# Causal scores, maxima and masks contracted over 32 rows of the array instead of 64

## The reference

```
q, k, v = split(x @ w_qkv);  q, k rotated by position
att = (q @ k^T) * 8**-0.5            # per head, 1024 x 1024
att = where(causal, att, -max)
y = softmax(att) @ v;  x = x + y @ w_proj
```

## Time and profile before

| | |
|---|---|
| median of 3 runs | 667.92 us |
| lowest, highest | 662.89, 1288.06 us |
| span of the profiled execution | 665.4 us |
| PE busy | 603.9 us (91%) |
| DVE busy | 476.5 us (72%) |
| ACT busy | 348.3 us (52%) |
| POOL busy | 161.6 us (24%) |
| instructions | 12374 |

### The profile page before, as it was taken

One profiled execution on the slowest core, in us unless ns is written; L12 is line 12 of the kernel. 1 busy time (PEld: TensorE's weight loads), 2 busy tenths in 40 slices (PEclk: granted clock), 3 DMA queues, 4 the chain that ended last, 5 costly groups with the idle time before them and its releaser, 6 DMA issues. The chain is left out here.

```text
span 665.4 us, 12374 instructions
## 1 busy us (share of the span) xinstructions
PE 603.9 (91%) x4296; PEld 419.6 (63%) x4296; DVE 476.5 (72%) x1493; ACT 348.3 (52%) x713; POOL 161.6 (24%) x332
## 2 busy tenths in 40 slices
PE   1997789999989969999999999989999998999997
PEld 0876668788878855654545454545454535888887
DVE  5577866688786768958787878777888422876764
ACT  3855456322324644657676777755777674323321
POOL 7640524020033437702223121222120000000000
PEclk9998989999989996759999999995999987999999
DMA  8000000324322200000000000000000001333332
GB/s 292 4 0 1 1 0 1 91 85 126 119 66 86 75 1 1 1 0 1 2 1 1 1 2 2 1 1 1 1 1 1 1 1 66 88 122 117 120 122 75
DMA packets 18669, 27.98 MB, mean 42 GB/s; under 512 B 2984, under 2 KB 7208, under 8 KB 18608
## 3 DMA queue, kind: packets, MB, share of 16 engines
q1 hardware_dynamic: 17888, 25.85, 12.2%
q10 hardware_dynamic: 720, 1.34, 0.6%
HBM read 25.85 MB, written 1.33 MB: 41 GB/s over the span
## 5 line engine op out<-in xcount | busy, mean ns | idle before, releaser
L831 ACT ACTIVATE arena<-bank 128x512 f32<-128x512 f32 (+3 forms) x384 | 166.7, 496 | 76.6 <-PE bank L1664 51.6
L1686 PE MATMUL bank<-kza,qta 64*128 64x512 f32 (+3 forms) x384 | 141.7, 447 | 7.0 <-DVE work L1201 3.5
L1198 DVE CUSTOM_DVE_ANT_0 bank<-bank,mask_qk 128x512 f32<-128x512 f32 (+3 forms) x256 | 119.5, 517 | 36.7 <-PE bank L1686 36.3
L1652 PE MATMUL bank<-qtb,kza 64*128 64x512 f32 (+3 forms) x384 | 138.1, 431 | 4.4 <-ACT arena L831 2.2
L1686 PEld LDWEIGHTS bank<-kza,qta 64*128 64x128 f32 x384 | 67.3, 204 | 84.9 <-DVE work L1198 45.5
L761 ACT ACTIVATE work<-bank 128x512 f32<-128x512 f32 x80 | 47.8, 597 | 113.6 <-PE bank L1321 113.6
L1201 DVE TENSOR_REDUCE work<-bank 128x1 f32<-128x512 f32 x128 | 80.3, 683 | 17.0 <-PE bank L1686 17.0
L1124 DVE TENSOR_TENSOR work<-work,bank 128x512 f32<-128x512 f32 x80 | 54.8, 685 | 47.4 <-PE bank L1321 42.6
L1609 PE MATMUL bank<-arena 128*9 128x512 f32 (+3 forms) x768 | 86.7, 526 | 0.4 <-ACT arena L831 0.4
L1652 PEld LDWEIGHTS bank<-qtb,kza 64*128 64x128 f32 x384 | 67.7, 199 | 29.9 <-ACT arena L831 18.1
L1540 PE MATMUL bank<-dw,work 128*128 128x128 f32 x640 | 85.7, 278 | 0.7 <-DVE work L1128 0.7
(11 more groups left out here) (193 smaller groups left out, 1053.0 us busy)
## 6 DMA issues: line engine op xcount, KB each, us to landing
kt<-cw_rows SPq DMA_DIRECT2D x160, 128.0 KB, 2.9
x<-x_in SPq DMA_DIRECT2D x4, 256.0 KB, 7.6
y_out<-x SPq DMA_DIRECT2D x4, 256.0 KB, 3.2
arena<-gw_in SPq DMA_DIRECT2D x1, 640.0 KB, 9.8
arena<-uw_in SPq DMA_DIRECT2D x1, 640.0 KB, 8.6
dw<-dw_in SPq DMA_DIRECT2D x1, 640.0 KB, 9.5
work<-q_in SPq DMA_DIRECT2D x2, 256.0 KB, 8.1
arena<-const_in ACTq DMA_DIRECT2D x1, 400.0 KB, 7.3
```

The lines of the kernel that those rows point to most:

```text
L831: act.activation(pb[:, blk % 2, h, 0:w], s_bank(n)[:, 0:w], ACT.Exp, scale=SCALE).then_inc(p_ready, 1)
L1198: ins = dve.tensor_tensor_reduce(out=src, in0=src, in1=mask_qk[:, CW - w:], scale=1.0, scalar=-3e38, op0=ALU.add, op1=ALU.max, accum_out=dst)
L1652: ins = pe.matmul(s_bank(n)[:, 0:w], kz(s, h, j // CT)[pair(h), j % CT * P:(j % CT + 1) * P], qtb[pair(h), s % 2, (c + 1) * CW - w:(c + 1) ...
L1686: pe.matmul(a_bank(n)[:, 0:w], qta[pair(h), slot(b, g), i * P:(i + 1) * P], kz(s, h, half)[pair(h), 0:w], start=True, stop=True).then_inc( ...
```

## The change

Scores and maxima contract over a head's own 32 rows, straight from `kt`. `kza`, its two memsets, all copies by `alone` on ACT and POOL, and all waits for `kz_ready` are gone. The four heads use four row parts of the array. The orders of the heads and `BLOCK_ORDER` change with it. The mask is now four slices of 32 columns contracted over 32 rows, in place of two slices of 64 over 64, so `mask_kq` is twice as wide, the input of constants grows from 800 to 1056 columns, and there are 1024 mask matmuls in place of 512. The masks of the heads of order 0 and 1 are written as one group, slice by slice in turn. `gb` is a tile of its own.

```
-S_HEADS, A_HEADS = (0, 2, 1, 3), (2, 0, 3, 1)
-BLOCK_ORDER = (("score", 0), ("max", 0), ("max", 1), ("score", 1), ("mask", 0), ("mask", 1), ("score", 2),
-               ("max", 2), ("mask", 2), ("sums", None), ("max", 3), ("score", 3), ("mask", 3))
+S_HEADS, A_HEADS = (0, 1, 2, 3), (2, 3, 0, 1)
+BLOCK_ORDER = (("score", 0), ("max", 0), ("score", 1), ("max", 1), ("mask", (0, 1)), ("score", 2), ("max", 2),
+               ("mask", (2,)), ("sums", None), ("score", 3), ("max", 3), ("mask", (3,)))
...
-    for h in range(GH):
-        put("act", -1, 3, "alone", 0, 1, h)
-        put("act", -1, 7, "alone", 1, 1, h)
...
-    for s in range(2, STEPS):
-        put("pool", s - 2, 7, "alone", s, 0)
-        put("pool", s - 1, 0, "alone", s, 1)
...
-    for h in range(GH):
-        put("act", c2 + 16, "alone", 0, 0, h)
-        put("act", c2 + 18, "alone", 1, 0, h)
...
-        kza = sb("kza", [P, 4, 2, CW], F32R)
-        gb = kt[:, G:G + 2, :].bitcast(F32).rearrange("p g (a n) -> p (g a) n", a=2)
+        gb = sb("gb", [P, 4, CW])
...
-        def pair(h):
-
-            return slice(h // 2 * 2 * SL, (h // 2 + 1) * 2 * SL)
+        def own_rows(h):
+
+            return slice(h * SL, (h + 1) * SL)
...
-                if r == NC:
-                    sp.wait_ge(kz_ready[STEPS - 2], 2 * GH)
-                    sp.wait_ge(kz_ready[STEPS - 1], 2 * GH)
...
-                    ins = pe.matmul(s_bank(n)[:, 0:w], kz(s, h, j // CT)[pair(h), j % CT * P:(j % CT + 1) * P],
-                                    qtb[pair(h), s % 2, (c + 1) * CW - w:(c + 1) * CW], start=True, stop=True)
+                    r = own_rows(h)
+                    ins = pe.matmul(s_bank(n)[:, 0:w], kt[r, slot(b, g), j * P:(j + 1) * P],
+                                    qtb[r, s % 2, (c + 1) * CW - w:(c + 1) * CW], start=True, stop=True)
...
+                    for a in range(GH):
+                        for order in orders:
+                            n = (s * NBLK + k) * GH + order
+                            r = own_rows(S_HEADS[order])
+                            ins = pe.matmul(s_bank(n)[:, a * SL:(a + 1) * SL], mask_kq[r, a, :], identb[r, r],
                                             start=False, stop=True, skip_group_check=True)
+                            if a == GH - 1:
+                                ins.then_inc(b_full, 1)
...
-                    if order == 0 and k in (0, 8):
-                        pe.wait_ge(kz_ready[s], GH * (1 + half))
...
-                    pe.matmul(a_bank(n)[:, 0:w], qta[pair(h), slot(b, g), i * P:(i + 1) * P],
-                              kz(s, h, half)[pair(h), 0:w], start=True, stop=True).then_inc(a_full, 1)
+                    r = own_rows(h)
+                    pe.matmul(a_bank(n)[:, 0:w], qta[r, slot(b, g), i * P:(i + 1) * P],
+                              kt[r, slot(b, g), half * CW:half * CW + w], start=True, stop=True).then_inc(a_full, 1)
```

More of the change, by code:

```diff
@@ L49 @@
 W_Q, W_KV, W_QKV, W_R, W_END = 0, 128, 384, 768, 786
-C_ID, C_MA, C_MB, C_BM, C_HS, C_IO, C_COS, C_SIN, C_END = 0, 128, 256, 512, 640, 656, 672, 736, 800
+C_ID, C_MA, C_MB, C_BM, C_HS, C_IO, C_COS, C_SIN, C_END = 0, 128, 256, 768, 896, 912, 928, 992, 1056
 S_S1, S_B1, S_GA, S_BE, S_CW, S_CB, S_END = 0, 4, 8, 9, 10, 13, 14
@@ L216, in macaron @@
         identb = sb("identb", [P, P], BF16)
-        mask_kq = sb("mask_kq", [P, 2, P], BF16)
+        mask_kq = sb("mask_kq", [P, GH, P], BF16)
         mask_qk = sb("mask_qk", [P, CW], BF16)
@@ L339, in macaron @@
             sem("qkv_full"), sem("qkv_ready"), sem("v_ready"))
-        stg_clear, kz_ready = sem("stg_clear"), [sem(f"kz_ready{s}") for s in range(STEPS)]
+        stg_clear = sem("stg_clear")
         kt_full, kt_ready = sem("kt_full"), sem("kt_ready")
@@ L368, in slot @@
             return G * b + (g + 2) % G
-        def kz(s, h, half):
-            return kza[:, 2 * (s % 2) + half, h % 2, :]
-        def pair(h):
-            return slice(h // 2 * 2 * SL, (h // 2 + 1) * 2 * SL)
+        def own_rows(h):
+            return slice(h * SL, (h + 1) * SL)
         def lin_bank(b, n):
@@ L517, in tile @@
                 pool.wait_ge(v_ready, n + 1)
[L519 to L531, removed]
             def negate(s, half):
@@ L556, in _ @@
             pool.memset(stm[:, :, :, :, :].bitcast(F32), 0.0)
-            pool.memset(kza[:, 0:2, :, :].bitcast(F32), 0.0)
             rstd(0)
@@ L577, in _ @@
             pool.tensor_copy(mask_qk[:, CW - P:], raw_c[:, C_MA:C_MA + P])
-            pool.tensor_copy(mask_kq[:, :, :], raw_c[:, C_MB:C_MB + 2 * P].rearrange("p (a n) -> p a n", a=2))
+            pool.tensor_copy(mask_kq[:, :, :], raw_c[:, C_MB:C_MB + GH * P].rearrange("p (a n) -> p a n", a=GH))
             pool.tensor_copy(bmask[:, :], raw_c[:, C_BM:C_BM + P + H])
@@ L610, in _ @@
                             negate(*todo[1:])
-                        if todo[0] == "alone":
-                            alone(*todo[1:])
                         if todo[0] == "norm":
@@ L802, in maxima @@
                 act.activation(qtb[:, s % 2, tok(half)], T[:, :], ACT.Copy).then_inc(qtb_ready, 1)
[L804 to L814, removed]
             def causal():
@@ L1285, in _ @@
             moments(0)
-            dve.memset(kza[:, 2:4, :, :].bitcast(F32), 0.0)
             moments(1)
@@ L1651, in score, with mask @@
                         pe.wait_ge(p_ready, n - S_DEEP + 1)
-                    ins = pe.matmul(s_bank(n)[:, 0:w], kz(s, h, j // CT)[pair(h), j % CT * P:(j % CT + 1) * P],
-                                    qtb[pair(h), s % 2, (c + 1) * CW - w:(c + 1) * CW], start=True, stop=True)
+                    r = own_rows(h)
+                    ins = pe.matmul(s_bank(n)[:, 0:w], kt[r, slot(b, g), j * P:(j + 1) * P],
+                                    qtb[r, s % 2, (c + 1) * CW - w:(c + 1) * CW], start=True, stop=True)
                     if j < 4 * c:
                         ins.then_inc(b_full, 1)
-                def mask(s, k, order):
+                def mask(s, k, orders):
                     c, j = B_BLOCKS[k]
[L1660 to L1664, removed]
+                    if j < 4 * c:
+                        return
+                    for a in range(GH):
[3 more added lines that the diff above has]
+                            ins = pe.matmul(s_bank(n)[:, a * SL:(a + 1) * SL], mask_kq[r, a, :], identb[r, r],
                                             start=False, stop=True, skip_group_check=True)
-                        ins.then_inc(b_full, 1)
+                            if a == GH - 1:
+                                ins.then_inc(b_full, 1)
                 def score_max(s, k, order):
@@ L1748, in constants @@
     c[:, C_MA:C_MA + P] = np.where(r[None, :] > r[:, None], -1e30, 0.0)
-    for a in range(2):
-        c[:, C_MB + a * P:C_MB + (a + 1) * P] = np.where(r[None, :] > (r[:, None] % (2 * SL) + a * 2 * SL), -1e30, 0.0)
+    for a in range(GH):
+        c[:, C_MB + a * P:C_MB + (a + 1) * P] = np.where(r[None, :] > (r[:, None] % SL + a * SL), -1e30, 0.0)
     c[:, C_BM:C_BM + P] = r[:, None] // HD == r[None, :] // HD
```

## The result

The changed kernel takes 732.54 us (median of 5 runs, 731.39 to 742.83), the kernel before 662.89 us (median of 5). The ratio is 1.1107, with a 95% interval from 1.1003 to 1.1211: slower by 11%; it is taken over the fast executions of each kernel, and one execution of before took 1288.06 us. The forecast was 661 us. The profiled execution of the changed kernel has a span of 739.4 us, 74.0 more than that of before.

A forecast was written before the change was run, and what follows sets the result against it. It took DVE's work as each step's floor (26.28 of 31.45 us), with PE and DVE pacing different blocks. From the 665.4 us span, - 7.1 + 1.9 - 2.5 + 3 gave 660.7, stated as 661; the 8-in-10 range was 641 to 684.

The forecast's parts named there:

- What bounds the kernel: Causal steps: DVE's 26.28 of 31.45 us is the floor, 5.2 us can be gained; PE and DVE set the pace by turns.
- part 1: Scores and maxima off the diagonal: four row parts save one 0.34 us slot in three blocks of seven steps, 7.1 us.
- rival A: Whole kernel: DVE paces everything, only the removed copies count, 663 us; 0.46 together with the forecast.
- rival B: Steps 0 to 6: DVE's waits halve as PE runs ahead, slots save more at half clock; 645 us, chance 0.27.
- Part 2: Diagonal blocks: more mask rounds at 0.04 us cancel the saved slot in steps 0 to 6 and cost 1.9 us in step 7.
- Rival D: Masks: the weight load comes ahead of each round, rounds 0.1 us apart; 679 us, chance 0.08.
- Part 3: Copies: without ACT's copies the Silu at the end of MOE0 no longer waits; 2.5 us saved, POOL's copies give nothing.
- Part 5: Clock: PE streams for less time, so falls get more frequent; one more long fall added, 3 us.
- Rival C: Causal stage: idle PE makes clock falls the rule; 682 us with five more, 700 us at half clock throughout; chance 0.13.

The follow-up runs named there:

- e5: Changed kernel with the masks of before (two slices of 64 columns over 64 rows), scores and maxima still over 32 rows: 760.29 us (2 runs).
- e3: Changed kernel with the head orders and block order of before, still contracting over 32 rows: 751.56 us, ratio 1.134.
- m1: Kernel of its own without the computation: six stretches, two 512-column slots per beat, differing only in rows at work; 128 rows held full clock, 64 or 32 fell to half.
- g1: Changed kernel with two zero-operand matmuls over 128 rows added ahead of each group of sums but the first of a half: 774.09 us (2 runs).
- g2: As g1, with the added matmuls over 32 rows in place of 128: 829.14 us (2 runs).
- f2: Changed kernel with every score of the causal stage computed twice, maxima once: 823.22 us (2 runs).
- m3: Third kernel of its own without the computation, six other stretches; the same 64-row work without a pause ran twice, taking 60.0 and 32.9 us.
- e6: Kernel before with only the maxima contracting over 32 rows, straight from the keys: 918.3 us, ratio 1.386.
- m2: Second kernel of its own without the computation, six other stretches; 128 rows with 9 columns held the clock, four 32-row parts with one slot per beat fell to 0.56.

## Why the prediction was wrong, point by point

**What bounds the kernel, and part 1.** The four parts start together, and the slot is saved where I said. But the sum of 7.1 us was wrong: 15.10 against 15.03 us and 10.60 against 10.59 for the same blocks at full clock show nothing left, and both `yout` blocks that I counted are among them. The block with `maxima` never ran wholly at full clock in the changed kernel, so it isn't measured. DVE is busy for 13.18 of 15.10 us and 13.20 of 15.03, so the saving presumably ends in a wait for DVE. That is rival A, for blocks at full clock. At half clock the 0.89 us less in the first blocks of step 0 are what rival B said of that stretch.

**Part 2.** At full clock four mask rounds last 0.26 us at 444.97 with 0.19 for one, 0.02 to 0.03 each after the first, not 0.04; small either way. Rival D's 0.1 us isn't there, and e5 shows that the masks aren't the cause.

```profile
444.97 0.26 PE L1616 MATMUL bank<-identb,mask_kq 32*128 32x32 bf16 x4
```

**Part 3.** The wait is gone as forecast: the Silu follows its product directly. That the sums begin 2.35 us earlier, near the 2.5 forecast, is in part luck. The first maximum of the pass ahead of step 0 starts 3.8 us earlier (246.98 against 250.74), and the pass then takes 1.4 us longer, 36.51 us at clock 0.50 against 35.10 at 0.69. The row of the Silu:

```profile
236.83 0.60 ACT L727 ACTIVATE work<-bank 128x512 f32<-128x512 f32 x1 [0.16 <-PE bank L1270]
```

**Part 5 is the step that failed**, in its reason and in its size. I wrote that the clock would fall oftener because PE streams for less time, and priced one more fall at 3 us. e3 streams its pairs for the old time and falls as far; m1 and the pair g1 and g2 show that the rows at work count, with the streamed time the same. The contraction over 32 rows halves the rows in every score and maximum, in all blocks of all steps, so this was no matter of one more fall: the cost is 75.6 us from the sums of step 0 on. I had rows 9 in front of me, and read them as "PE pauses". The place in the trace of before with fewer rows at work was the pass ahead of step 0, where the maxima run without scores: there the clock was 0.69, from 250.74 to 285.84, with PE busy for 32.99 of 35.10 us. I took that for DVE's pace alone. Part 5 also left out the fall at 248.0, and with it the question of how soon a lost clock comes back.

**Rival C** had the place (the clock) and the wrong mechanism, with 0.13. Its price was low as well: it took 16.82/11.91 = 1.41 for a step at half clock, but that stretch had a mean clock of 0.63. Step 6 takes 46.80 us at 0.50 against 31.07 before at 1.00, which is 1.51. And I believed only half of the 82 us that the rival gave at most. The measured 732.54 us lie 48.5 above the upper end of 684.

**Not settled.** f2 wasn't forecast by the theory that the other runs bear out; that its clock stays lost as in m3 is argued, not shown, and g2, which loses every return of the changed kernel by more 32-row streams, is as open. So is what makes the clock return within the steps of the changed kernel at all. No run contracts over 64 rows without the copies, so their absence is excluded only by m1, where no copies are made in any stretch and the clock still goes by the rows. Whether e6 is at half because of its rows or because of its pauses at each change of form stays open.

## What to carry to other kernels

A matmul that contracts over fewer rows streams its columns in the same time, but that doesn't make the change free. Where matmuls over parts of the array run fewer than four at a time, ask how many rows are at work on the average before and after, and look in the present profile for stretches with few rows and a full PE record. Zero padding that looks like waste (64 rows where 32 hold data) is part of what kept this kernel at 2.4 GHz for most of its time, a mean clock of 0.940 against 0.785. And when a lower clock makes a bound stage take 1.5 times as long, its rival deserves more than the price of one fall taken from one profile.

## What the runs showed of the hardware

- A full PE column says nothing of the clock: it was 1.00 and 0.52 for the same 64-row work with a record of 32.88 of 32.90 and 59.99 of 60.00 us (m3). The Trainium skill (TensorE: Matmul & The Clock Gate, Why this matters for your kernels) asks for TensorE to be kept busy, without long idle gaps between bursts of matmuls, so that the clock doesn't drop. Idle PE ahead of the falls at 243.3 and 248.0 agrees with that. The first stretch of m3 doesn't: it fell to half with PE busy for 2.19 of 2.20 us before, and the pause of 0.8 us between the 70 matmuls and the stretch stands ahead of the second stretch too, which held. So here gaps alone don't tell.
- Rows and streamed time both count: 2 slots in a beat held 1.00 over 128 rows and fell over 64 (0.53 to 0.54, m1), and over 128 rows 1 slot fell to 0.56 (m2, m3).
- A lost clock can stay lost: 57.8 us of 64-row work without a pause stayed at half in m3, and the same work held full clock for 32.9 us where it wasn't lost.
- Stationary columns don't matter for it: 9 columns held like 128 (m2).
- Scores over 64 rows and maxima over 32 didn't run side by side: 0.72 us from one start to the next at half clock, and 918 us for the kernel (e6).
